# Joining the W products of two groups into one visit, pairs 0 to 5

## The reference

```
A  = tril(q k^T) * scale              128 x 128
ok = enz * (A es)                     128 x 64 slots, es = exp(s), enz = exp(-z)
qv = softmax(ok)
W2 = tril((qv * enz) es^T)            128 x 128, contracted over the 64 slots
o  = W2 v                             128 x 128
y += (rmsnorm(o) * g_norm * silu(g)) Wo
```

## Time and profile before

| | |
|---|---|
| median of 3 runs | 604.72 us (604.59 to 605.63) |
| span of the profiled execution | 601.8 us |
| PE, PEld busy | 575.6 us (96%), 486.0 us (81%) |
| DVE, ACT, POOL busy | 485.0 us (81%), 371.2 us (62%), 281.9 us (47%) |
| granted clock of TensorE, mean | 0.996 |
| HBM read, written | 17.55 MB, 1.05 MB |

### The profile page before, as it was taken

The page is one execution under the profiler, slowest core; times in us unless marked ns, Lnnn a source line. Parts: engine busy times, 40 slices in busy tenths (PEclk is TensorE's granted clock), DMA queues, the critical chain, the costliest instruction groups (busy, mean ns, idle before and its releaser), DMA issues. The chain is left out here.

```text
span 601.8 us, 14128 instructions
## 1 busy us (share of the span) xinstructions
PE 575.6 (96%) x4426; PEld 486.0 (81%) x4426; DVE 485.0 (81%) x1150; ACT 371.2 (62%) x1168; POOL 281.9 (47%) x324
## 2 busy tenths in 40 slices
PE   5989999999999999999999999998789999999997
PEld 5868888888888888888888788886568878877786
DVE  6999978977977986987987798677587887887766
ACT  3438557657657567556655576676867567567453
POOL 3367754845764663764575566355762211210000
PEclk9999999999999999999999999999999999999999
DMA  8200201100200200200200000232000000000000
GB/s 277 71 0 5 85 0 36 54 2 10 78 0 0 87 0 0 87 0 0 83 4 0 19 3 1 89 92 103 3 3 11 3 11 11 3 11 11 4 10 17
DMA packets 10096, 19.34 MB, mean 32 GB/s; under 512 B 2112, under 2 KB 5696, under 8 KB 9920
## 3 DMA queue, kind: packets, MB, share of 16 engines
q1 hardware_dynamic: 10048, 18.73, 9.2%
HBM read 17.55 MB, written 1.05 MB: 31 GB/s over the span
## 5 line engine op out<-in xcount | busy, mean ns | idle before, releaser
L884 ACT ACTIVATE sa_v<-bank 128x256 f32<-128x256 f32 x64 | 24.5, 382 | 60.8 <-PE bank L268 60.8
L857 ACT ACTIVATE sa_ex<-sa_okb,sa_minus_top 128x64 f32<-128x64 f32 x128 | 42.9, 340 | 28.7 <-DVE sa_minus_top L750 26.7
L947 POOL TENSOR_TENSOR sa_qt<-sa_rope_cos,sa_rope_sin 128x512 f32<-128x512 f32 x32 | 41.1, 1286 | 39.1 <-DVE sa_rope_sin L798 38.1
L266 PE MATMUL bank<-ht_hi,sa_qk_hi 128*128 128x512 f32 x128 | 55.2, 432 | 1.3 <-DVE sa_gate L803 0.9
L947 POOL TENSOR_TENSOR sa_kt<-sa_rope_cos,sa_rope_sin 128x512 f32<-128x512 f32 x32 | 41.2, 1286 | 26.6 <-DVE sa_rope_sin L798 26.6
L266 PE MATMUL bank<-sa_vg_hi,ht_hi 128*128 128x512 f32 x128 | 53.0, 414 | 0.5 <-DVE sa_rope_sin L798 0.5
L268 PE MATMUL bank<-sa_vg_hi,ht_lo 128*128 128x512 f32 x128 | 50.5, 395 | 0.0
L267 PE MATMUL bank<-sa_vg_lo,ht_hi 128*128 128x512 f32 x128 | 50.5, 395 | 0.0
L268 PE MATMUL bank<-ht_hi,sa_qk_lo 128*128 128x512 f32 x128 | 50.5, 394 | 0.0
L796 DVE TENSOR_TENSOR sa_rope_cos<-bank,con 128x512 f32<-128x512 f32 x64 | 43.9, 686 | 7.9 <-PE bank L268 6.8
L267 PE MATMUL bank<-ht_lo,sa_qk_hi 128*128 128x512 f32 x128 | 50.2, 392 | 0.0
(11 more groups left out here) (207 smaller groups left out, 1830.1 us busy)
## 6 DMA issues: line engine op xcount, KB each, us to landing
sa_qk_raw<-in_wqk SPq DMA_DIRECT2D x8, 512.0 KB, 3.8
sa_vg_raw<-in_wvg SPq DMA_DIRECT2D x8, 512.0 KB, 3.3
sa_wo_raw<-in_wo SPq DMA_DIRECT2D x8, 256.0 KB, 2.6
xf_w_raw<-in_w SPq DMA_DIRECT2D x2, 640.0 KB, 9.0
xf_w_raw<-in_w SPq DMA_DIRECT2D x1, 1152.0 KB, 7.4
xs<-in_x SPq DMA_DIRECT2D x2, 512.0 KB, 4.7
hn<-in_w SPq DMA_DIRECT2D x2, 512.0 KB, 4.6
out<-xs SPq DMA_DIRECT2D x8, 128.0 KB, 1.7
```

What stands on the lines that cost most here:

```text
L266: pe.matmul(out, w_hi, m_hi, start=first, stop=False)
L857: ins = act.activation(ex[:, s, u, :], okb[:, s, u, :], ACT.Exp, bias=minus_top[:, s, u:u + 1], accum_out=total[:, buffer_of(i, g, 4), u:u ...
L947: pool.tensor_tensor(dst[:, h, c * HALF:(c + 1) * HALF], rope_cos[:, s, :], rope_sin[:, s, :], ALU.add).then_inc(roped, 1)
```

## The change

A new step W2 n replaces W 2n and W 2n + 1 in the tables of turns 0 to 5. On TensorE it makes the products of both groups in one visit, 8 of them, heads alternating: head 0 of both groups fills ps_w (four blocks of 128 columns), head 1 of the even group goes to ps_o[0], of the odd group to ps_o[1]. It waits for qet of both groups and for both O banks. On VectorE, W2 is one instruction of 512 columns and two of 256. Pairs 6 and 7 keep W. The orders of turns 0 to 5 are set anew on all four engines.

```diff
-ATTENDING = {("A", 0): (2,), ("E", 0): (3,), ("T", 0): (4,), ("W", 0): (5, 6), ("W", 1): (7,), ("O", 0): (6,), ("O", 1): (7,)}
+ATTENDING = {("A", 0): (2,), ("E", 0): (3,), ("T", 0): (4,), ("W2", 0): (5, 6, 7)}
...
+                elif step == "W2":
+                    first = 2 * n
+                    pe.wait_ge(qet_done, at(i, first + 1))
+                    pe.wait_ge(es_t_done, 2 * i + n + 1)
+                    pe.wait_ge(w2_done, at(i, first, 1))
+                    pe.wait_ge(og_done, at(i, first, 1))
+                    for u in range(8):
+                        g, b, h = first + u // 4, 2 * first + u // 2, u % 2
+                        rows, half = slice(h * SLOTS, (h + 1) * SLOTS), u // 2 % 2
+                        out = ps_w[:, u // 2 * TOK:(u // 2 + 1) * TOK] if h == 0 else ps_o[g % 2][:, half * TOK:(half + 1) * TOK]
+                        mm = pe.matmul(out, es_t[rows, b * TOK:(b + 1) * TOK], qet[rows, g % 2, half, :], start=True, stop=True)
+                    mm.then_inc(w_ready, 2)
...
+                elif step == "W2":
+                    dve.wait_ge(w_ready, at(i, 2 * n + 1))
+                    dve.wait_ge(o_ready, at(i, 2 * n, 1))
+                    dve.tensor_tensor(w2t[:, :, :, 0, :].rearrange("p s b c -> p (s b) c"), bank(ps_w, 0, 512, 4),
+                                      tri.unsqueeze(1).to_broadcast([P, 4, TOK]), ALU.mult)
+                    for s in range(2):
+                        dve.tensor_tensor(w2t[:, s, :, 1, :], bank(ps_o[s], 0, 256, 2),
+                                          tri.unsqueeze(1).to_broadcast([P, 2, TOK]), ALU.mult).then_inc(w2_done, 1)
```

More of the change, by code:

```diff
@@ L134 @@
 PE_ORDER = [("A", 0), ("QK", 0), ("A", 1), ("E", 0), ("SN", 0), ("ST", 0), ("A", 2), ("E", 1), ("QK", 1), ("E", 2),
[4 rows of a table removed]
-DVE_ORDER = [("A", 0), ("QK", 0), ("A", 1), ("E", 0), ("SN", 0), ("ST", 0), ("A", 2), ("E", 1), ("QK", 1),
[4 rows of a table removed]
-ACT_ORDER = [("W2P", 0), ("VGHI", 0), ("E", 0), ("SN", 0), ("T", 0), ("E", 1), ("E", 2), ("T", 1), ("O", 0),
[3 rows of a table removed]
-POOL_ORDER = [("QK", 0), ("VGLO", 0), ("E", 0), ("E", 1), ("WO", 0), ("QK", 1), ("E", 2), ("QK", 2), ("SUM", 0),
-    ("MS", 0), ("E", 3), ("QK", 3), ("SN", 0), ("SUM", 1), ("MS", 1), ("QK", 4), ("WOLO", 0), ("SUM", 2),
-    ("SUM", 3), ("MS", 2), ("QK", 5), ("MS", 3), ("SN", 1), ("QK", 6), ("QK", 7), ("QKLO", 0)]
[4 rows of a table added]
+DVE_ORDER = [("A", 0), ("QK", 0), ("A", 1), ("E", 0), ("SN", 0), ("ST", 0), ("A", 2), ("E", 1), ("QK", 1), ("E", 2),
[4 rows of a table added]
+ACT_ORDER = [("W2P", 0), ("VGHI", 0), ("E", 0), ("SN", 0), ("E", 1), ("T", 0), ("E", 2), ("T", 1), ("O", 0), ("T", 2),
[3 rows of a table added]
+POOL_ORDER = [("WO", 0), ("VGLO", 0), ("QK", 0), ("SUM", 0), ("E", 0), ("E", 1), ("QK", 1), ("QK", 2), ("E", 2),
+    ("MS", 0), ("E", 3), ("QK", 3), ("WOLO", 0), ("SUM", 1), ("SN", 0), ("MS", 1), ("QK", 4), ("SUM", 2), ("MS", 2),
+    ("QK", 5), ("SUM", 3), ("MS", 3), ("SN", 1), ("QK", 6), ("QK", 7), ("QKLO", 0)]
 H_PE = [("QK", 0, -1), ("QK", 1, -1), ("VG", 0, -1), ("VG", 1, -1), ("VG", 2, -1), ("VG", 3, -1), ("VG", 4, -1),
     ("QK", 2, -1), ("SN", 0, -1), ("SN", 1, -1), ("QK", 3, -1), ("VG", 5, -1), ("ST", 0, -1), ("ST", 1, -1),
[8 rows of a table removed]
[8 rows of a table added]
 H_DVE = [("RA", 0, -1), ("VG", 0, -1), ("VG", 1, -1), ("QK", 0, -1), ("QK", 1, -1), ("VG", 2, -1), ("VG", 3, -1),
[1 row of a table removed]
[1 row of a table added]
     ("VG", 6, -1), ("QK", 4, -1), ("QK", 5, -1), ("QK", 6, -1), ("A", 0, 0), ("QK", 7, -1), ("ST", 0, -1),
     ("VG", 7, -1), ("ST", 1, -1), ("A", 1, 0), ("E", 0, 0), ("QK", 0, 0), ("SN", 0, 0), ("A", 2, 0), ("E", 1, 0),
[5 rows of a table removed]
-H_ACT = [("VG", 0, -1), ("VG", 1, -1), ("VG", 2, -1), ("VG", 3, -1), ("RS", 0, -1), ("W2P", 0, -1), ("VG", 4, -1),
[6 rows of a table removed]
-H_POOL = [("QK", 0, -1), ("QK", 1, -1), ("QK", 2, -1), ("WO", 0, 0), ("QK", 3, -1), ("SN", 0, -1), ("QK", 4, -1),
[4 rows of a table removed]
[5 rows of a table added]
+H_ACT = [("VG", 0, -1), ("VG", 1, -1), ("RS", 0, -1), ("VG", 2, -1), ("W2P", 0, -1), ("VG", 3, -1), ("VG", 4, -1),
[6 rows of a table added]
+H_POOL = [("WO", 0, 0), ("QK", 0, -1), ("QK", 1, -1), ("QK", 2, -1), ("QK", 3, -1), ("SN", 0, -1), ("QK", 4, -1),
[4 rows of a table added]
 PROJECTING = {"QK", "VG", "ST", "SN", "CS", "W2P", "VGHI", "VGLO", "QKHI", "QKLO"}
```

## The result

The changed kernel takes 609.62 us, median of 4 runs (608.74 to 610.27), against 604.65 for the kernel before (604.23 to 605.63): ratio 1.008 [1.0062, 1.0098], slower by 5.0 us. The execution profiled here is the one at 610.27, the slowest of the four; its span is 608.5.

What follows compares the result with a forecast made beforehand. TensorE's own list of steps was taken to set the pair's length, with VectorE lacking slack in its first third. Five loop turns at 0.75 (3.75) and pair 0 at 1.0 add 4.75 to 604.72: 609.5 us, own range 607.3 to 612.

Steps and rivals of the forecast that it cites:

- turn 0: Pair 0, with tables of its own and the same joined visits: 1.0 us longer, bounds 0.3 and 1.8.
- share for handovers: Some eight engine handovers from QK 1 to the second visit: pair's loss taken as 0.75, between 0.5 without them and 1.1.
- The visit's price: Joined W visit on TensorE takes 1.09 instead of twice 0.65; with entry effects 0.35 saved per visit gone, 0.70 a pair.
- First wait, QK 4: TensorE waits about 0.6 at QK 4, because VectorE reads the joined visit and E 3 before QK 3.
- Second wait, VG 2: VectorE idles for rms before O 0, so QK 5 is read late and TensorE waits 0.4 at VG 2.
- The third chain: From T 3 through ScalarE and GpSimd to O 1 on VectorE: holds the second joined visit until 216.9 in the trace.
- The second visit: Second joined W visit starts 28.88 after the pair's start without handovers, with 19.61 from there to the pair's end.
- the swaps of the prologue: Few steps swapped ahead of A 0 (RS, RT, WO, QK 6): counted at nothing, some tenths if their cover is gone.
- That the gain holds: Rival: no new wait is left at QK 4 or the second visit; 4.2 us gained, 600.5 us, chance 0.12.
- that half the waits aren't real: Rival: path through rms is shorter, so the 0.6 at QK 4 and the 0.70 gain cancel; 604.5 us, chance 0.07.
- more waits than these: Rival: VectorE falls behind in pair 0 and handovers are long, 1.3 a pair and 2 there; 613 us, chance 0.07.
- The rule of the skill: Packing speeds up TensorE but not PSUM reading: VectorE needs 1.27 for the joined visit against 1.32 before.

Runs made afterwards that it cites:

- cheap rms: Changed kernel with the power that makes rms replaced by a product in turns 0 to 5 (results not the reference's): 608.32 us, ratio 1.0065.
- light QK 3: Changed kernel with VectorE reading QK 3 by two instructions instead of three in the loop (results not the reference's): 609.44 us, ratio 1.0091.

## Why the prediction was right, point by point

The forecast was 609.5 us and slower; 609.62 were measured. The direction and the two waits that make it were reasoned and came as reasoned. That the time agrees to 0.1 us is in part luck: turn 0 was 0.8 too low, the turns count 5.5 us where the medians differ by 5.0, and the share for handovers was a choice between 0 and 0.6. Its steps:

**The visit's price** was right: 1.09 from start to start, 1.16 long. On VectorE it takes 1.26 (157.81 to 159.07), for 1.27.

**First wait, QK 4.** Predicted 0.6, measured 0.43. QK 4 itself starts where the prediction put it, right behind VectorE's reading of QK 3: 19.37 after the turn's start, for 19.4. The wait is smaller because TensorE comes there 0.2 later than worked out.

**Second wait, VG 2.** Predicted 0.4, measured 0.64, and VectorE's idle time before O 0 is 0.93 where 0.56 was worked out (207.34 to 207.9). VectorE was done with QK 3 at 19.31 after the turn's start, for 19.32 worked out; what was late is O 0 on VectorE, 20.24 for 19.88. The squares (1.22) and rms (1.29, 161.37 to 162.66) took what their rows said; the 0.36 are O 0 on TensorE, whose rows begin and end 0.1 to 0.2 later, and the handover from rms, 0.21 for 0.1. The two waits sum to 1.07, for 1.0 predicted. The stretch up to the second visit lost 1.37 in all (counted under turn 0 below); the other 0.30 is spread over steps that start 0.05 to 0.15 late, O 0 to T 2 0.98 for 0.89, for instance. The prediction had this only as its share of 0.25 for handovers, and no experiment takes it apart. That the holds are not independent, the kernels with one or both shortened show: 0.00, 0.35 and 0.63 a turn.

**The third chain** ended where it was put: O 1 on VectorE ends at 171.57, 28.94 after the turn's start, for 28.88. Whether it would hold the visit there by itself is not shown. With both holds shortened the turn fell to 48.10, below the 48.49 that this chain was to set, but the cheap rms shortens the chain as well (MS 1 is in it), and the light QK 3 starts it earlier. The other orders moved its steps along with all others.

**The second visit** started at 29.10, for 28.88 without handovers and 29.13 with the share of them that was taken. From there to the end are 19.64, for 19.61. So the turn grew by 0.73, for 0.75: 3.7 us of the 3.75.

**Turn 0 was mis-sized**: 1.0 predicted with bounds 0.3 and 1.8, 1.83 measured. The two kernels side by side; first the one before, at QK 1, W 3 and the next turn's start:

```profile
51.37 0.50 PE L266 MATMUL bank<-ht_hi,sa_qk_hi 128*128 128x512 f32 x1
...
73.88 0.71 PE L612 MATMUL bank<-sa_qet,sa_es_t 64*128 64x128 f32 x8
...
92.11 1.05 PE L572 MATMUL bank<-sa_qt,sa_kt 128*128 128x128 f32 x8
```

then the changed one, from QK 1 on, with the rows where TensorE stands:

```profile
51.57 0.50 PE L266 MATMUL bank<-ht_hi,sa_qk_hi 128*128 128x512 f32 x1
...
57.90 1.16 PE L615 MATMUL bank<-sa_qet,sa_es_t 64*128 64x128 f32 x16 [0.23 <-issue]
...
65.42 0.50 PE L266 MATMUL bank<-ht_hi,sa_qk_hi 128*128 128x512 f32 x1 [0.35 <-DVE sa_rope_sin L820]
...
69.26 0.50 PE L266 MATMUL bank<-sa_vg_hi,ht_hi 128*128 128x512 f32 x1 [0.25 <-DVE sa_rope_sin L820]
...
74.37 1.16 PE L615 MATMUL bank<-sa_qet,sa_es_t 64*128 64x128 f32 x16
```

Up to QK 1 only 0.20 was lost, so counting the swaps of the prologue at nothing was nearly right. From QK 1 to the visit before VG 3 are 22.80, against 22.51. Out of that stretch went O 2 (0.88), three visits of 0.65 for one of 1.09 (0.86), and two entries (0.22): 20.55 was due, so 2.25 are waits. The same count in the loop gives 29.69 less 1.96, 27.73 due, 29.10 measured, 1.37 of waits. (Behind the visit come 1.34 more, for the O 2 and the longer visit that now lie there, 1.32; 0.20, 0.29 and 1.34 are the 1.83.) Turn 0 thus waits 0.88 more than a loop turn: by the distances between starts some 0.3 at the first visit, 0.3 at VG 0, 0.5 at QK 4, 0.4 at VG 1 and 0.2 at VG 2. VectorE shows where this begins. Its table for turn 0 has the visit ahead of QK 2, the loop's behind it. So VectorE stands 1.05 for the visit, and reads QK 2, which TensorE had written by 57.7, only from 60.37 on; in the kernel before it began with QK 2 at 58.60:

```profile
59.09 0.69 DVE L768 TENSOR_TENSOR sa_w2t<-bank,con 128x512 f32<-128x512 f32 x1 [1.05 <-PE bank L615]
```

```profile
58.60 0.68 DVE L796 TENSOR_TENSOR sa_rope_cos<-bank,con 128x512 f32<-128x512 f32 x1
```

The visit itself comes late also because ScalarE copies T 1 for it only at 57.19, behind the steps of CS 1 and a load of its function table (1.28, from 55.90). No run moves these steps, so this is read from the trace and not tested. The term took turn 0 for a loop turn with 0.25 on top, and did not look at this order.

**The rivals.** That the gain holds (600.5) falls with the two waits; that half the waits aren't real (604.5) falls with 1.37 lost to waits and late starts for a gain of 0.70; more waits than these (613) fits turn 0 alone.

**The rule of the skill** on which the direction was argued was the Trainium skill, TensorEngine Tiling (Array Packing), PSUM Bottleneck: packing speeds up TensorE, not the reading of PSUM. The runs go further than the rule. Reading was not made longer by the join, 1.26 for two visits; it was put in one piece ahead of QK 3, and the visits that stood between one fill and the fill that reuses its bank, during which VectorE had caught up, were taken away. With W 2 and O 2 back in their places the wait at VG 2 is gone, and that fits one join costing 0.16 to 0.35 a turn and both 0.85. That it is these two steps, and not the order laid out with them, is argued from kernels with different tables, not shown by moving one step.

## What to carry to other kernels

Where two engines pass banks to each other in written orders, a short step of the faster one between a fill and its bank's next use can be cover for the slower one; before joining two steps, write down for each fill when its bank is read, and count only what is left. The holds that come up are to be taken as a chain: shortening the reading ahead of QK 4 alone gave nothing, the path through rms alone 0.35 us a turn, both 0.63. A table written out by hand for one turn deserves the same look as the loop's: turn 0 lost 1.8 us, two and a half times a loop turn. And a new order should be measured without the change it was made for: here it was worth 0.35 us a turn, and no join earned anything on top of it.

## What the runs showed of the hardware that was not expected

Behind turn 5 all kernels run the same tables, and still that part took 268.96 to 271.10 us. First the whole of it in the changed kernel and the two places where it differs (from:to, length, five engines, granted clock, DMA):

```profile
337.40:608.50 271.10, 255.90 (x2391) 211.45 (x2390) 207.74 (x579) 172.84 (x506) 91.29 (x122) 0.98 0.07 22
...
436.00:439.00 3.00, 0.59 (x7) 0.39 (x6) 1.99 (x5) 2.41 (x7) 1.58 (x3) 1.00 0.02 5
...
442.00:445.00 3.00, 3.00 (x20) 1.66 (x20) 2.54 (x13) 2.69 (x7) 0.00 (x0) 0.50 0.00 0
...
563.00:567.00 4.00, 4.00 (x56) 3.32 (x55) 3.00 (x6) 0.62 (x2) 0.00 (x0) 0.57 0.01 4
```

then the same places in the kernel with turn 0 of before:

```profile
335.64:604.60 268.96, 251.97 (x2391) 208.19 (x2390) 207.48 (x579) 172.83 (x506) 91.29 (x122) 1.00 0.07 23
...
434.20:437.20 3.00, 0.59 (x7) 0.38 (x5) 2.00 (x5) 2.42 (x7) 1.57 (x3) 1.00 0.02 5
437.20:440.20 3.00, 2.77 (x32) 2.36 (x32) 0.80 (x3) 2.33 (x7) 1.65 (x2) 1.00 0.00 0
...
560.20:564.20 4.00, 3.60 (x62) 2.99 (x63) 3.97 (x8) 0.62 (x2) 0.00 (x0) 1.00 0.02 4
```

Both kernels run the same steps here, and TensorE is as little busy in both ahead of the first place, 0.59 of 3.00 us. In the first its granted clock then fell to 0.50, the 1.2 GHz level; in the second it stayed at 2.4 GHz. It is the same at the second place, after 0.70 of 2.00 us in both. Set side by side, the starts of TensorE's steps in this part differ by under 0.1 up to the first place, by 1.1 behind it and by 2.1 behind the second: that is the whole difference of a part in which nothing was changed. The profiled execution of the kernel before has the first fall and not the second, and so its 1.2 against the changed kernel. The changed kernel's profiled run (mean clock 0.991, 610.27 us) lies for the same reason above its run of 608.74 at 0.997, and the kernel without joins shows spans of 599.6 at 0.997 and 602.0 at 0.991. What decides whether the clock falls, no run here shows. With a change worth 1 to 2 us, spans are to be compared by the stretch that was changed, and medians together with the mean clocks of their runs.
